# Moving the second halves of the split probabilities behind the last mask, the last unit's transposes early, and half an output projection ahead of a query projection

## The reference, cut to what matters

```python
q = einsum('bsd,ed->bse', x, Wq)      # 32 heads of 128
k = einsum('bsd,ed->bse', x, Wk)      # 8 heads of 128
v = einsum('bsd,ed->bse', x, Wv)
q, k = rmsnorm(q) , rmsnorm(k)        # then both are rotated by their positions (rope)
k_all = concat([k_cache[block_table], k])     # 512 cached + 128 new keys
v_all = concat([v_cache[block_table], v])
scores = where(valid, einsum('bqhd,bkhd->bhqk', q, k_all) / sqrt(128), -1e30)
probs = softmax(scores)
o = einsum('bhqk,bkhd->bqhd', probs, v_all)
x = x + einsum('bse,de->bsd', o.reshape(b, s, 4096), Wo)
```

## Time and profile before

| | |
|---|---|
| median of 3 runs | 1334.36 us |
| the profiled execution's own time | 1333.57 us |
| its span, first to last instruction | 1332.0 us |
| PE busy | 1297.4 us (97%) |
| PEld, DVE, ACT, POOL busy | 83%, 73%, 59%, 57% |
| mean granted TensorE clock | 0.992 of full speed |
| DMA | 178 MB, mean 134 GB/s |

### The profile page before, as it was taken

The page is one execution under the profiler, slowest core; times in us unless marked ns, Lnnn a source line. Parts: engine busy times, 40 slices in busy tenths (PEclk is TensorE's granted clock), DMA queues, the critical chain, the costliest instruction groups (busy, mean ns, idle before and its releaser), DMA issues.

```text
span 1332.0 us, 25952 instructions
## 1 busy us (share of the span) xinstructions
PE 1297.4 (97%) x6728; PEld 1102.7 (83%) x6728; DVE 972.5 (73%) x2500; ACT 779.8 (59%) x1829; POOL 756.7 (57%) x778
## 2 busy tenths in 40 slices
PE   8999999997999999999999999999999999999997
PEld 8888888886888888788888878888888787888886
DVE  5532344978778877978777788888777878777883
ACT  5731334455566667576666666666566666656663
POOL 3100000257666668776666686766667876666662
PEclk9999999998999999999999999999999999999998
DMA  7321214176555557756555577555557665555533
GB/s 259 130 63 48 71 48 128 52 261 185 121 123 122 125 127 199 182 124 136 127 132 128 141 186 188 121 134 139 131 120 182 178 159 116 121 122 122 122 90 79
DMA packets 314845, 178.01 MB, mean 134 GB/s; under 512 B 260752, under 2 KB 279568, under 8 KB 314512
## 3 DMA queue, kind: packets, MB, share of 16 engines
q1 hardware_dynamic: 296128, 126.88, 39.9%
q0 software_dynamic: 11264, 32.77, 9.8%
q10 hardware_dynamic: 7376, 17.45, 4.0%
HBM read 118.15 MB, written 16.91 MB: 101 GB/s over the span
## 4 chain that ended last, share of the span: by engine, by line
PE 79%; DVE 6%; ACT 4%; issue 4%; POOL 2%; SPq 2%; DMA 1%; ACTq 0%; DVEq 0%; POOLq 0%
PE bank L1555 15%; PE tail L1593 15%; PE wide L1623 12%; PE tail L1657 11%; PE wide L455 4%; PE wide L1587 4%; PE wide L531 3%; PE bank L1576 3%; PE bank L455 2%; PE tail L455 2%; PE wide L583 2%; DVE parts L1968 1%; PE bank L531 1%; ACT prT L1758 1%; POOL wq1T L1303 1%
## 5 line engine op out<-in xcount | busy, mean ns | idle before, releaser
L1593 PE MATMUL tail<-prT,vt 128*128 128x512 f32 x960 | 266.3, 416 | 8.9 <-POOL prT L1349 2.8
L1593 PEld LDWEIGHTS tail<-prT,vt 128*128 128x128 f32 x960 | 173.8, 193 | 55.5 <-DVE prT L1957 12.5
L1286 POOL TENSOR_TENSOR tick<-tick 128x1 f32<-128x1 f32 x254 | 55.8, 220 | 270.6 <-PE tail L1593 91.6
L1657 PE MATMUL tail<-woT,oT 128*128 128x512 f32 x768 | 179.7, 390 | 0.8 <-DVE oT L2008 0.8
L1657 PEld LDWEIGHTS tail<-woT,oT 128*128 128x128 f32 x768 | 144.1, 188 | 31.1 <-DVE oT L2008 1.2
L1623 PE MATMUL wide<-kT,qT 128*128 128x320 f32 x512 | 158.8, 310 | 2.0 <-DVE mx L1984 1.5
L1623 PE MATMUL wide<-kT_low,qT 128*128 128x320 f32 x512 | 158.4, 309 | 0.0
L1623 PE MATMUL wide<-kT,qT_low 128*128 128x320 f32 x512 | 158.1, 309 | 0.0
L1786 ACT ACTIVATE pr<-pr,nm,q_scale 128x640 f32<-128x640 f32 x128 | 118.0, 922 | 42.7 <-DVE nm L1987 42.2
L1786 ACT ACTIVATE raw<-raw,nm,q_scale 128x640 f32<-128x640 f32 x124 | 114.7, 925 | 44.7 <-DVE nm L1987 43.5
L1340 POOL TENSOR_TENSOR parts<-raw,parts 128x1280 f16<-128x1280 f32 x50 | 132.4, 2647 | 7.3
(11 more groups left out here) (280 smaller groups left out, 2912.4 us busy)
## 6 DMA issues: line engine op xcount, KB each, us to landing
w_ring<-pair_weights SPq DMA_DIRECT2D x80, 256.0 KB, 4.3
k_raw<-k_pages SPq DMA_DIRECT2D x512, 32.0 KB, 1.7
v_raw<-v_pages SPq DMA_DIRECT2D x512, 32.0 KB, 2.8
spread<-one_over_denominators ACTq DMA_DIRECT2D x32, 512.0 KB, 4.6
xTb<-x_transposed POOLq DMA_DIRECT2D x31, 512.0 KB, 4.2
rope<-rope_tables SPq DMA_DIRECT2D x31, 256.0 KB, 2.8
out<-y POOLq DMA_DIRECT2D x31, 256.0 KB, 4.9
w_raw<-w_gate_up SPq DMA_DIRECT2D x10, 512.0 KB, 3.3
```

The lines of the kernel that those rows point to most:

```text
L1286: nc.gpsimd.tensor_tensor(tick[:, 2:3], tick[:, 1:2], tick[:, 1:2], ALU.add).then_inc(s_carry, 1)
L1593: last = nc.tensor.matmul(tail[g][:, :], vt[v_part][:, j, g * D:(g + 1) * D], prT[p_part][:, :, j, :], start=(j == v_part == p_part == 0), ...
L1657: last = nc.tensor.matmul(place[:, :], oT[:, g, o_part, (h % REP) * S:(h % REP + 1) * S], woT[w_part][:, h, :], start=(h == o_part == w_pa ...
```

## The change

The rests that VectorE makes no longer stand between its masks (two after mask 5, two after mask 7): all four stand behind mask 7. In the last turn that has masks (unit 31), GpSimd leaves the rests of k=1 to VectorE. In the first turn GpSimd splits the values before it casts the first probabilities, and splits one output weight chunk fewer ahead of that. In the first turn of pairs 1 to 3, TensorE does the first 12 matmuls of the output projection ahead of the second query projection. In the last turn of all, TensorE transposes the probabilities of key head 1 before it waits for the DMA transposes, and then does the 15 sums of key head 0 in one piece; ScalarE waits with its copies for the first ten of them (new semaphore `s_ph`), VectorE with its own for all fifteen.

```diff
@@ gpsimd turn
-                low_weights(own, 3 * KT, 3 * KT + 3)
+                low_weights(own, 3 * KT, 3 * KT + 2)
                 for i in range(2):
                     pool.wait_ge(m_full[i], B // 2)
                 pool.wait_ge(s_xlast, 16 * (B // 4))
-                halve(u, n, 0, True, False)
-                split_values(u, n + 1, True)
-                halve(u, n + 2, 1, True, False)
-                low_weights(own, 3 * KT + 3, 4 * KT)
+                split_values(u, n, True)
+                for k in range(2):
+                    halve(u, n + 1 + k, k, True, False)
+                low_weights(own, 3 * KT + 2, 4 * KT)
...
-                halve(u, n + 2, 1, False, not extra)
+                halve(u, n + 2, 1, False, not extra and then_x is not None)
@@ tensor_engine turn
-            if front:
-                project(0, wqT[1], ready=chunks_done(pair, 2 * KT) if first_turn else None)
...
+            behind_next = share and front and isinstance(b, int) and b == 0
+            if behind_next:
+                output(tail[1], w, 0, REP)
+            if front:
+                project(0, wqT[1], ready=chunks_done(pair, 2 * KT) if first_turn else None)
...
             if share:
                 pe.wait_ge(s_wlo, ...)
-                output(tail[1], w, 0, REP)
+                if not behind_next:
+                    output(tail[1], w, 0, REP)
                 output(tail[1], w, REP, REP).then_inc(s_y, 1)
+            if back and not front:
+                for w in range(2):
+                    probs_wide(1, w)
+                transposes(0, probs_of(1, JT - 1))
             if back:
                 pe.wait_ge(s_tl, u * 2 + 2)
...
-                sums(0, range(JT), (0, 1), 0)
-                sums(0, (0, 1), (0,), 1)
-                probs_wide(1, 0)
+                highs = sums(0, range(JT), (0, 1), 0)
+                if front:
+                    sums(0, (0, 1), (0,), 1)
+                    probs_wide(1, 0)
+                else:
+                    highs.then_inc(s_ph, 1)
+                    sums(0, range(JT), (0,), 1).then_inc(s_pv, 1)
@@ scalar turn, high_probs
                 act.wait_ge(t_full[w], u + 1)
+                if not front:
+                    act.wait_ge(s_ph, 1)
@@ vector turn, low_probs
+                if not front:
+                    dve.wait_ge(s_pv, u * G + 1 + FIRST)
@@ vector turn, after the masks
-                    if (extra or not back) and h in (REP + 1, HP - 1):
-                        for i in range(HALF):
-                            rest_of((h - REP - 1) // 2 * HALF + i)
+                for h in range(0 if extra or not back else REP if ahead else HALF, REP):
+                    rest_of(h)
```

More of the change, by code:

```diff
@@ L1133, in build_attention @@
     s_xt = sem("xTb_loaded")
+    s_ph = sem("last_high_sums_done")
     s_ropel = sem("rope_loaded")
@@ L1639, in turn @@
                 project(1, wqT[0], ready=chunks_done(pair, KT))
-            if front:
-                project(0, wqT[1], ready=chunks_done(pair, 2 * KT) if first_turn else None)
-            if not back:
-                rest.third_quarter()
-                rest.fourth_rows()
             def output(place, of, h0, m):
@@ L1683, in turn @@
                 transposes(0, [ra[:, REP + i, :] for i in range(G)])
-            if back:
+            if back and front:
                 sums(0, (2, 3), (0,), 1)
@@ L1689, in turn @@
                 rotated = full[1].value()
-            if back:
+            if back and front:
                 sums(0, (JT - 1,), (0,), 1).then_inc(s_pv, 1)
                 transposes(0, probs_of(1, JT - 1))
+            if back:
                 pe.wait_ge(s_yadd, u + FIRST)
```

3 lines of the change are left out of this document (added).

## The result

The changed kernel takes 1346.5 us (median of four runs, 1344.0 to 1347.8); the kernel before, in four runs beside it, 1334.7 (1334.0 to 1335.9). The ratio is 1.0090, 95% interval 1.0071 to 1.0109: 12 us slower. The forecast was 1335.0 with a range to 1339.5, so it was wrong, and on the side of its slower rival. The profiled execution took 1347.1 us, its span 1345.1, at a mean granted clock of 0.986.

What follows compares the result with a forecast made beforehand. TensorE, busy 1297.4 of 1332.0 us, was taken as the bound. Terms -4.9 + 2.6 + 2.1 + 0 + 1.0 = +0.8 on 1333.57 gave 1334.4, adjusted for the runs' median to 1335.0 us, range 1329.0 to 1339.5.

Steps and rivals of the forecast that it cites:

- slower rival: Rival C: half clock behind gathered waits at the changes of pair, about 1340 us, chance 0.16.
- changes of pair: Three turns: wait for `wq1T` only moves before the query transpose, `low_turned(1)` ends as before; 0 us, bounds ±0.5 each.
- "out" turns: Three turns: late rests delay the DMA transposes, so TensorE's value sums start later; +2.1 us in all.
- clock: TensorE behind new gaps: one half-clock stretch of 1.7 us at less than even odds; +1.0 us, ends 0 and 5.
- first unit: First gap shrinks, but late rests delay `high_turned(1)` and so the value sums; +2.6 us, bounds -3.4 and +4.
- last unit: Earlier rests, gap filled with transposes, value sums at full clock; -4.9 us, bounds -5.3 and -2.4.
- smallest gain, -2.4: Last unit's weaker bound: gain of 2.4 us if TensorE's clock there is still at half.
- Four rests alternate with a cast and two chunks: Changes of pair: VectorE's rests and GpSimd take turns from 534.4, ending at 540.9, against 540.59 before.
- Rival C: Changes of pair: 2.5 us wait in one piece brings half clock, 5.1 us, first unit 0.7 more; about 1340, chance 0.16.
- B: Rests slip through without strict alternation and transposes overlap: 1327 to 1330 us; sign, rests at 0.81 us; chance 0.26.
- D: Last unit stays at half clock and gains 2.4 instead of 4.9 us: 1337.5 us, chance 0.12.

Runs made afterwards that it cites:

- rests_out: Kernel before with only the rests of the three "out" turns moved behind the last mask; 1339.8 us, ratio 1.0028.
- reordered: Kernel before with rests of six turns behind the last mask and SyncE's DMA transposes there issued high, high, low, low; 1335.7 us, ratio 1.0010.
- rests_next: Kernel before with only the rests of the three turns at the end of a pair moved behind the last mask; 1337.5 us, ratio 1.0012.
- half_alone: Kernel before with only the half output projection ahead of the second queries in turns behind a change of pair; 1335.2 us, ratio 1.0014.
- all_parts: The whole change timed once more in many runs against the kernel before; 1343.0 us, ratio 1.0065.
- last_alone: Kernel before with only the last turn changed: early transposes, two new waits, last two rests on VectorE; 1332.2 us, ratio 0.9983.

## Why the prediction was wrong, step by step

What failed is the forecast for the turns in which the rests moved, and for the clock behind them. It put the three changes of pair at nothing, the "out" turns at +2.1 and the clock at +1.0. In the trace of the changed kernel, the steps by which the first value sums of a unit come later than before are:

| part | forecast | trace | alone, in many runs |
|---|---|---|---|
| first unit (sums of units 0, 1) | +2.6 | +3.0 | +2.0 |
| changes of pair (7, 8; 15, 16; 23, 24) | 0 | +6.5 (3.5, 2.9, 0.0) | rests +1.6, half projection +1.9 |
| "out" turns (9, 10; 17, 18; 25, 26) | +2.1 | +8.3 (3.6, 1.7, 3.0) | +3.7 |
| clock | +1.0 | within the other rows | |
| last unit, to the end | -4.9 | -4.8 | -2.3 |
| sum (the trace's span: 1345.1 - 1332.0) | +0.8 | +13.1 | |

- **Last unit, -4.9: mis-sized, measured -2.3.** The mechanism is right: no gap, full clock, a trace shorter by 4.25 + 0.48 = 4.7 us. But 2.8 us of it were a stretch at half clock that two of the ten traces with the old turn show in full, five in part and three not at all; it was taken for certain. Against that one trace the -4.9 came out; against many runs it is too large. That the forecast's smallest gain, -2.4, is the measured value is chance: it stood for a new turn that stays at half clock, and the new turn ran at full clock.
- **"Out" turns, +2.1: mis-sized, measured +3.7 alone.** The step that failed is the time at which the second transpose can go out, and what three in a row then take. In unit 9 the forecast had both first rests done at 604.0; the second transpose went out at 611.35 - 6.55 = 604.80, since the first rest took 2.0 us and the second another 0.8. The forecast had the last one there 6.5 us behind that; it took 618.49 - 611.35 = 7.1, the three issues alone 4.82 with their gaps. So `low_turned(1)` ends 1.4 us later than said and the query transpose stands 3.1 us late instead of 1.6. Then, in this trace, TensorE runs at half clock; in rests_out the mean clock is no lower than before (0.9910 against 0.9912), so its +3.7 is waiting. reordered shows that this queue is the path.
- **Changes of pair, 0: wrong for the whole change.** "Four rests alternate with a cast and two chunks, ending at 540.9": they don't have to alternate. The last ended at 544.14 - 3.04 (the delay of that turn's start) = 541.1, near enough, but the first two, which release the transpose, at 542.67 - 3.04 = 539.6. The forecast asked when the last rest ends; the queue asked when the second does. `low_turned` then ends 2.3 us later than before (551.05 - 3.04 against 545.70), where the forecast had it as before, and TensorE's wait is 5.37 us where the forecast had some 2.5. Of the 5.37, 3.7 are work that TensorE has done sooner (its output projection ends at 545.74 - 3.04 instead of 546.38), and 1.85 is how much later the query transpose starts. Alone, rests_next costs 1.6 and half_alone 1.9, and neither interval excludes 0.
- **First unit, +2.6: fits**, measured +2.0 alone, with an interval that holds 0 too, and +3.0 in the trace; the wait before `wq1T` shrank to 2.37 us and the one behind it grew, as said. Its first and longer piece, 6.86 us before the query transpose, was ended by `low_turned`; the second, 2.26 us before the value sums, by `high_turned`, which was over at 324.72, as the forecast had it.
- **Clock, +1.0: mis-sized, some 4 to 6.** By the slope above it is some 4 us in all_parts (0.9875 against 0.9915), and some 6 in the profiled run (0.986 against 0.992), both estimates. Rival C had the effect at 5.8 for the changes of pair and the first unit, with a chance of 0.16. It was right that such gaps bring half clock, and left out the "out" turns; the trace after has a stretch in units 7, 9, 15 and 25. By these estimates the clock is about half of the loss, and waiting the rest.
- **B and D fell.** The rests do take 0.81 us more often than before (median 814 ns, before 1546), the sign that the forecast had named for B, and the time rose all the same: what counts is the end of the second and the fourth rest, not the median. D's condition, half clock in the last unit, didn't come (1.00).

## What to carry to other kernels

When a producer is moved later in its engine's order, the instant that matters is when it releases the next entry of an in-order queue, not when its last instruction ends: the low transpose of the first half held up a high one that had long been ready, and putting the ready ones first won back 7 of 8.5 us of that part. A gap on the bounding engine can be priced twice, by its length and by the clock behind it, and gathering short waits into one long one can cost by itself; filling the gap with work that nobody needs gave the clock back and not the time. And one trace is one throw: a gain that rests on a stretch at half clock must be weighed by how often other traces show that stretch.

## What the runs showed of the hardware that was not expected

**One engine's queue can pass the other's waiting instruction several times over.** The kernel last_alone, where the code of unit 23 is that of the kernel before; VectorE, GpSimd, TensorE:

```profile
1047.16 7.54 DVE L1986 TENSOR_TENSOR parts<-raw,parts 128x640 f16<-128x640 f32 x2 [0.61 <-POOL parts L1338]
...
1047.07 2.57 POOL L1304 TENSOR_TENSOR wq1T<-w_ring,wq1T 128x512 fp32r<-128x512 f32 x2
1049.58 0.80 POOL L1287 TENSOR_TENSOR tick<-tick 128x1 f32<-128x1 f32 x1
1050.32 1.24 POOL L1338 CAST parts<-raw 128x1280 f16<-128x1280 f32 x1
1051.53 2.49 POOL L1304 TENSOR_TENSOR wq1T<-w_ring,wq1T 128x512 fp32r<-128x512 f32 x2
...
1063.36 1.11 PE L1577 MATMUL bank<-ident,ra 128*128 128x128 f32 x4 [2.87 <-DVE rs L1942]
```

Two rests took 3.2 and 4.5 us, where the same two took 3.73 together in the kernel before. A rest of 4.5 us stands in seven of the traces, always at the end of a pair and behind a cast and two chunks; when it comes and when the engines take turns, the traces don't tell. The Trainium skill has it that who issues first holds the ports for the whole instruction ("SBUF — State Buffer", "Who interferes with whom"). The lengths agree with that, but in these seven traces the next to go is GpSimd again, three instructions in a row, while the rest waits.

**A named releaser can be a fellow sufferer.** A VectorE instruction of ten columns takes 0.17 us, and 1.1 to 1.3 beside the GpSimd copy that really ended TensorE's wait; it ends with that copy, so the profile names it as the last. A constant lag behind the same instruction in several traces (here 0.06 and 0.24 us), and the condition in the code, tell the two apart.

**The same code isn't the same time.** Up to unit 26 last_alone runs the code of the kernel before, and its sums of unit 26 stand 6.4 us later: 1.4 in the first two units, where twelve sums took 5.46 instead of 4.43 us, 0.7 at the first change of pair, 0.7 at unit 9, 0.5 at unit 17, and 3.3 by the two long rests above and the half clock behind them.
